# Cross-attention with a mixture-of-experts layer on one core: the value product written in head order, transfers given to other halves, four gate stores issued by ScalarE

## The reference

```python
q = (lat @ Wq) * scale                       # lat: layer norm of x, 64 queries a sequence
k, v = kv_in @ Wk, kv_in @ Wv                # kv_in: 64 context rows and the 64 rows of lat
alphas = softmax(where(mask, q @ k.T, -inf)) # per sequence and head
x = x + (alphas @ v).reshape(...) @ Wo
scores = sigmoid(norm(x) @ gate_w)           # top 2 of 8, normalised: dense
h = silu(xt @ w1) * (xt @ w3)                # per expert
x = x + shared(xt) + sum_e dense[:, e] * (h_e @ w2_e)
```

## Time and profile before

| what | before |
|---|---|
| median of three runs | 1117.17 us (1116.64 to 1120.89) |
| the profiled execution: its own time | 1118.87 us |
| its span, first to last instruction | 1117.1 us |
| PE busy | 1076.3 us (96%) |
| DVE busy | 928.3 us (83%) |
| ACT busy | 789.0 us (71%) |
| POOL busy | 617.0 us (55%) |
| mean granted TensorE clock | 0.991 |

### The profile page before, as it was taken

How to read it: one execution, slowest core, us unless ns; L and a number is a source line. 1 busy time by engine, 2 the same in 40 slices (tenths; PEclk the granted TensorE clock), 3 DMA queues, 4 the chain that set the end, 5 groups by cost and what they waited for, 6 DMA issues and landing times.

```text
span 1117.1 us, 28209 instructions
## 1 busy us (share of the span) xinstructions
PE 1076.3 (96%) x7720; PEld 939.3 (84%) x7720; DVE 928.3 (83%) x4095; ACT 789.0 (71%) x2924; POOL 617.0 (55%) x717
## 2 busy tenths in 40 slices
PE   6899999999999999999999999999999999999986
PEld 5688888888888888888888888888888888888765
DVE  3878988888988888988888888888898888888856
ACT  4777777767777776777776777777777777777631
POOL 5554655565656565655555556556565556554421
PEclk9999999999999999999999999999999999999989
DMA  5454555555565545555555655555555554555541
GB/s 153 128 175 152 171 171 166 153 155 162 168 176 171 160 146 167 171 171 165 157 155 159 172 170 169 168 156 158 165 168 171 174 153 153 163 168 160 158 121 34
DMA packets 248717, 176.81 MB, mean 158 GB/s; under 512 B 29424, under 2 KB 215408, under 8 KB 248560
## 3 DMA queue, kind: packets, MB, share of 16 engines
q1 hardware_dynamic: 247376, 173.96, 52.6%
q10 hardware_dynamic: 1184, 1.05, 0.3%
HBM read 103.35 MB, written 71.56 MB: 157 GB/s over the span
## 4 chain that ended last, share of the span: by engine, by line
PE 61%; SPq 14%; DMA 9%; DVE 8%; issue 5%; ACT 2%; POOL 0%; DVEq 0%; POOLq 0%; ACTq 0%
PE bank L861 14%; PE bank L874 12%; PE bank L816 9%; PE bank L818 9%; PE bank L817 9%; SPq L335 8%; DMA pT<-probsT_dram 8%; PE bank L822 5%; SPq L328 2%; SPq L351 2%; DVE probsT L687 2%; DVE logits L672 1%; SPq L369 1%; ACT cT_hi L528 1%; ACT probs L558 1%
## 5 line engine op out<-in xcount | busy, mean ns | idle before, releaser
L454 POOL TENSOR_TENSOR probs<-probs,rdenom 128x512 f32<-128x512 f32 x256 | 266.7, 1042 | 339.8 <-DVE rdenom L681 335.4
L558 ACT ACTIVATE probs<-logits,neg_max 128x128 f32<-128x128 f32 x1024 | 398.8, 396 | 0.9 <-DVE neg_max L672 0.9
L874 PEld LDWEIGHTS bank<-kvT,tT 128*128 128x128 f32 x2048 | 268.9, 192 | 120.5 <-issue 102.2
L861 PE MATMUL bank<-pT,kv_f 128*128 128x512 f32 x512 | 267.5, 604 | 16.5 <-DMA pT<-probsT_dram 16.0
L874 PE MATMUL bank<-kvT,tT 128*128 128x128 f32 x2048 | 270.5, 275 | 0.0
L672 DVE CUSTOM_DVE_ANT_0 logits<-bank,mask_add 128x128 f32<-128x128 f32 x1024 | 232.5, 282 | 6.1 <-PE bank L874 5.9
L717 DVE TENSOR_TENSOR cT_lo<-bank,cT_hi 128x512 fp32r<-128x512 f32 x256 | 175.1, 684 | 60.5 <-ACT cT_hi L528 60.5
L528 ACT CAST cT_hi<-bank 128x512 fp32r<-128x512 f32 x256 | 150.1, 586 | 94.7 <-PE bank L861 94.6
L558 ACT ACTIVATION_READ_ACCUMULATOR probs<-logits,neg_max 128x1 f32 x1024 | 197.7, 193 | 0.0
L513 ACT ACTIVATE h_tanh<-bank 128x256 f32<-128x256 f32 x160 | 61.6, 385 | 179.1 <-PE bank L818 176.7
L687 DVE STREAM_TRANSPOSE probsT<-probs 128x512 f32<-128x512 f32 x256 | 175.9, 687 | 0.5 <-issue 0.5
(11 more groups left out here) (102 smaller groups left out, 1986.1 us busy)
## 6 DMA issues: line engine op xcount, KB each, us to landing
probsT_dram<-probsT SPq DMA_DIRECT2D x256, 256.0 KB, 2.2
pT<-probsT_dram SPq DMA_DIRECT2D x1024, 64.0 KB, 2.2
gates<-gates_dram SPq DMA_DIRECT2D x62, 256.0 KB, 4.2
kv_raw<-in_ctx SPq DMA_DIRECT2D x32, 128.0 KB, 2.8
kv_raw<-in_x SPq DMA_DIRECT2D x32, 128.0 KB, 2.9
mask_raw<-in_mask_BxS_ik SPq DMA_DIRECT2D x32, 128.0 KB, 3.7
x_res<-in_x SPq DMA_DIRECT2D x32, 128.0 KB, 2.6
out<-out_sb SPq DMA_DIRECT2D x32, 128.0 KB, 2.1
```

Source lines behind the costliest of these rows:

```text
L454: nc.gpsimd.tensor_tensor(by_pair, by_pair, rdenom[n][:, :].unsqueeze(2).unsqueeze(3).broadcast_to([P, PAIRS, P // QUAD, QUAD]), ALU.mult) ...
L558: nc.scalar.activation(probs[c % 4][:, :, r, :], logits[c % 2][:, r, :].rearrange("p (c k) -> p c k", k=QUAD), ACT.Exp, bias=neg_max[c % 2 ...
L861: nc.tensor.matmul(C_ps[c % 2][:, :], kv_f[g % 3][:, kl % 4, :], pT[c % 3][:, :], start=True, stop=True).then_inc(C_in_psum, 1)
L874: last = nc.tensor.matmul(S_ps[c % 2][:, P * r:P * (r + 1)], tT[:, kl % 4, hd:hd + 2, :], kvT[g % 2][:, kl % 4, :], start=True, stop=True)
```

## The change

The value product is written in head order where it is copied out: the copies read the bank as before and write 32 columns at a time to their head's place, so that a head's 64 queries are one run. The transfers of SP change their halves (key and value rows 7 to 2, mask 1 to 3, x 2 to 3, output 3 to 4, the gates' loads from half 0 of the next frame to half 7), and the four gate stores, in SP's halves 5 and 6, go to ACT's queue, to the end of half 6. The gates' loads in half 7 wait for the stores of the same frame.

```diff
         def head_columns(cT, hd):
-            hh, r, odd = hd // 8, hd % 8 // 2, hd % 2
-            return cT.rearrange("p b t (o a r q) -> p b t o a r q", o=2, a=2, r=PAIRS)[:, :, hh, odd, :, r, :]
+            return cT.rearrange("p b t (h q) -> p b t h q", h=8)[:, :, hd // 8, hd % 8, :]
+
+        def by_quad(row):
+            return row.rearrange("p (r a q) -> p a r q", r=PAIRS, q=QUAD)
...
-                    if k == 0 and has(j, p, 3, NG + 1):
-                        sp.wait_ge(gates_stored, 64 * (i - 2))
-                        after(sp, h_routed_done, NT * (i - 3))
+                    if k == 2 and has(j, p, -2, NG - 4):
+                        load_kv(j, p + 3)
+                    if k == 3 and has(j, p, -1, NG - 3):
+                        load_mask(j, p + 2)
...
+                    if k == 7 and has(j, p, 2, NG):
+                        sp.wait_ge(gates_stored, 64 * (i - 1))
+                        after(sp, h_routed_done, NT * (i - 2))
                         for a in range(2):
                             sp.dma_start(gates[FH * a:FH * (a + 1), :, :],
...
-                    if k in (5, 6) and has(j, p, 2, NG):
-
-                        sp.wait_ge(gate_step, GATE_STEPS * (i - 1))
-                        after(sp, gates_loaded, 32 * (i - 2))
-                        for a in (0, 1) if k == 5 else (2, 3):
-                            sp.dma_start(gates_dram.rearrange("e (t a q) -> e t a q", t=TT, a=P // QUAD)[:, :, a, :],
-                                         g_denseT[QUAD * a:QUAD * a + E, :, :]).then_inc(gates_stored, 16)
...
-                        nc.scalar.copy(cT_hi[g % 2][:, kl % 4, kl // 4, :], C_ps[c % 2][:, :]).then_inc(cT_hi_ready, 1)
+                        nc.scalar.copy(by_quad(cT_hi[g % 2][:, kl % 4, kl // 4, :]),
+                                       C_ps[c % 2][:, :].rearrange("p (a r q) -> p a r q", r=PAIRS, q=QUAD)).then_inc(cT_hi_ready, 1)
...
+                    if k == 6 and has(j, p, 2, NG):
+                        act.wait_ge(gate_step, GATE_STEPS * (i - 1))
+                        after(act, gates_loaded, 32 * (i - 2))
+                        for a in range(P // QUAD):
+                            nc.scalar.dma_start(gates_dram.rearrange("e (t a q) -> e t a q", t=TT, a=P // QUAD)[:, :, a, :],
+                                                g_denseT[QUAD * a:QUAD * a + E, :, :]).then_inc(gates_stored, 16)
...
-                        nc.vector.tensor_tensor(cT_lo[g % 2][:, kl % 4, kl // 4, :], C_ps[c % 2][:, :],
-                                                cT_hi[g % 2][:, kl % 4, kl // 4, :].bitcast(fp32),
+                        nc.vector.tensor_tensor(by_quad(cT_lo[g % 2][:, kl % 4, kl // 4, :]),
+                                                C_ps[c % 2][:, :].rearrange("p (a r q) -> p a r q", r=PAIRS, q=QUAD),
+                                                by_quad(cT_hi[g % 2][:, kl % 4, kl // 4, :].bitcast(fp32)),
                                                 ALU.subtract).then_inc(cT_lo_ready, 1)
...
-                            last = matmul3(W_ps.rearrange("p (b a q) -> p b a q", b=GB, a=2), MV_hi[1][:, hd, :], MV_lo[1][:, hd, :],
+                            last = matmul3(W_ps.rearrange("p (b q) -> p b q", b=GB), MV_hi[1][:, hd, :], MV_lo[1][:, hd, :],
```

More of the change, by code:

```diff
@@ L346, in frame @@
                         load_probs(e - 2)
-                    if k == 0 and has(j, p, 3, NG + 1):
-                        sp.wait_ge(gates_stored, 64 * (i - 2))
-                        after(sp, h_routed_done, NT * (i - 3))
+                    if k == 2 and has(j, p, -2, NG - 4):
+                        load_kv(j, p + 3)
+                    if k == 3 and has(j, p, -1, NG - 3):
+                        load_mask(j, p + 2)
+                    if k == 3 and has(j, p, 0, NG - 1):
+                        after(sp, x1_step, 3 * (i - 2) + 1)
+                        sp.dma_start(x_res[p][:, :, :],
+                                     x.rearrange("b s d -> (b s) d")[bass.ds(GT * i, GT), :].rearrange("(t q) d -> q t d", q=P)
+                                     ).then_inc(x_res_loaded[p], 16)
+                    if k == 4 and has(j, p, 4, NG + 2):
+                        store_out(i - 1)
+                    if k == 7 and has(j, p, 2, NG):
+                        sp.wait_ge(gates_stored, 64 * (i - 1))
+                        after(sp, h_routed_done, NT * (i - 2))
                         for a in range(2):
@@ L353, in frame @@
                                          ).then_inc(gates_loaded, 16)
[L354 to L363, removed]
-                    if k in (5, 6) and has(j, p, 2, NG):
-                        sp.wait_ge(gate_step, GATE_STEPS * (i - 1))
-                        after(sp, gates_loaded, 32 * (i - 2))
-                        for a in (0, 1) if k == 5 else (2, 3):
-                            sp.dma_start(gates_dram.rearrange("e (t a q) -> e t a q", t=TT, a=P // QUAD)[:, :, a, :],
-                                         g_denseT[QUAD * a:QUAD * a + E, :, :]).then_inc(gates_stored, 16)
-                    if k == 7 and has(j, p, -2, NG - 4):
-                        load_kv(j, p + 3)
                 if i == NG + 2:
```

## The result

The change takes 1110.82 us, the median of six runs (1109.57 to 1114.02); the kernel before, on the same chip, 1119.06 (1116.64 to 1122.62). The ratio is 0.9927, 95% interval 0.9906 to 0.9947: 8.2 us less, where 11.0 were forecast (1106 us, from the 1117.17 of the first three runs of before). The profiled execution took 1111.61 us with a span of 1109.8, 7.3 less than before.

A forecast was written before the change was run, and what follows sets the result against it. PE was taken to bound the kernel, with a steady wait for pT. Terms -11.7 - 1.5 - 3 + 4.0 + 1.2 = -11.0 us, from 1117.2 to 1106 us; range 1100 to 1119.

The forecast's parts named there:

- The gates' loads (-11.7): Gate loads moved to half 7 no longer delay half 1's pT; PE's whole wait for pT goes, -11.7 us.
- ScalarE's stores (0): Four gate stores on ACT, 2.94 us, start ahead of half 6's exponentials, so half 7's copy tT stays in time: price 0.
- Rivals 1 and 2: ACT's stores wait in order behind the exponentials: 1115 us at 0.70 us an issue (0.11), or dearer, 1131 us (0.12).
- rival 1: ACT's stores wait in order behind the exponentials, at 0.70 us an issue: +9.2, 1115 us; chance 0.11.
- 0.33 us of PE a frame, 28 frames: If stores wait for the exponentials, half 7's copy tT ends late and PE loses this much: 9.2 us.
- The break-even of 1.1 us an issue: ACT's four stores cost PE nothing in half 7 up to 1.1 us an issue, if started ahead of the exponentials.
- Rival 3: The pT wait only moves to half 2, gate loads blocking half 0's loads: 1116 us; chance 0.09.
- 1.2 to 1.9 us to spare: Margin by which half 0's pT, behind the moved gate loads, comes before PE wants it in half 2.
- Rival 4: ACT's and SP's issues take turns, four stores take 4.8 us, PE loses 0.24 us a frame: 1113 us; chance 0.05.
- The head order (-1.5): The projection's 1536 matmuls read runs of 64 instead of 32 columns: 0 to 3.1 us gained, -1.5 taken.
- The end (+2.2): Last frames: -3 from gate stores off SP, +4.0 from last stores behind ACT's tanh, +1.2 from a slower clock.
- The other moves: price 0: Key and value rows, mask and x loaded in halves 2 and 3, well before they are read: no cost.

The follow-up runs named there:

- Moves alone: The changed kernel with the value product back in the old column order, only the transfers moved: 1114.41 us, 0.9949 of the kernel before.
- Experiment 3: The changed kernel with the gates' two loads put back into half 0 of the next frame, ScalarE keeping the stores: 1118.04 us, 1.0004 of before.
- experiment 4: The changed kernel with the four gate stores back on SyncE's queue in halves 5 and 6: 1110.45 us, 0.9915 of before.
- experiment 5: The changed kernel with ScalarE's stores also waiting until the exponentials of half 6 are done: 1129.69 us, 1.0081 of before.
- Experiment 7: The changed kernel with VectorE's gate step g_keep moved behind the product h in half 4: 1103.81 us, 0.9878 of before.
- experiment 8: The changed kernel with the four gate stores of frame 32 alone issued by SyncE, in halves 5 and 6: 1103.47 us, 0.9875 of before.
- experiment 9: The kernel before, unchanged, profiled once more: 1117.11 us, a single run.
- experiment 11: The changed kernel with g_keep behind h, frame 32's stores on SyncE, and frames -2 to 0 loading in the old halves: 1096.51 us, 0.9818 of before.

## Why the prediction was right, and where it was off

**The gates' loads (-11.7) and ScalarE's stores (0): right.** Moves alone take 918.46 us for frames 3 to 30 (115.81 to 1034.27), 11.9 less than before. Experiment 3 shows that without the loads' new place the gain is gone, as the prediction argued, and experiment 4 that the queue of the stores is beside the point. That the two loads alone would give all of the 11.7 is not shown: experiment 3 puts their place at 7 to 9 us, and at 4.6 in its profiled execution. The stores start ahead of the exponentials, 0.67 to 0.69 us each in frame 13 (0.70 taken).

**Rivals 1 and 2** did not come; experiment 5 makes the queue behave as they assume, and there rival 1 was priced too low, 17 us instead of 9.2: the step "0.33 us of PE a frame, 28 frames" took frame 13 for all, and frames 2 and 3 lose several times that, frame 3 with the clock at 0.95. The break-even of 1.1 us an issue stood the test: eight issues, 5.6 us, are 1.2 us over 4.4, and the frames are 1.2 us longer. **Rival 3** did not come: between frames 3 and 31 PE has no wait for `pT` left. Its "1.2 to 1.9 us to spare" hold in most frames; in 7 of the 27 from 3 to 29 less is left, 0.65 us in the worst. Its 1116 us does not follow from the terms: without the -11.7 the others add up to +0.7, about 1118. In the same way the upper end of the sum's own bounds is -11.7 + 4.0 + 3.5 = -4.2, which is 1113 and not 1112; the measured median lies under both. **Rival 4** did not come either: it has each of ScalarE's issues take 1.19 us, and they took 0.67 to 0.69.

**The head order (-1.5) came to about -2, for another reason.** That the two are near is luck. "284 ns, the query chunk's 282: between 0 and 2 ns each" failed: the matmuls gained 7 ns, beyond what the nearest row allowed. Why they are now faster than the chunk's, no run here shows. 48 matmuls, started 114 instead of 120 ns apart, are 0.3 us a frame, 8 us in 28 frames. Of it 0.05 arrived: the wait for `h` took 0.20, a bound that the prediction did not look for, since a PE that arrives later than the product shows no wait for it. Experiment 7 gave it back, and a little more.

**The end (+2.2) measured +2.5, of larger pieces; that their sum came out so near is luck.** From frame 31 to the tanh of half 6 it gained 5.3 us (1095.96 - 1042.73 against 1080.94 - 1032.97) where -3 was taken: both the wait and the slower clock of frame 32 went. From the tanh to the expert sums it lost 5.4 instead of 4.0: the stores left 4.0 us later, as said, and the two loads landed later as well. From there to the end it lost 2.3 instead of 1.2, with the clock at 0.50 for the expert sums. In experiment 8 the late stores are gone and the end takes 69.26 instead of 76.83 us, so they cost both losses.

**"The other moves: price 0" and the first frame with gates failed by 1.1 and 1.2 us.** At the start the key and value loads stand ahead of half 5's `pT`; that this costs the 1.1 us is a guess (experiment 9), which no edit shows, as experiment 11 is too small. In frame 2 there are no expert sums yet, PE is early, and the copy behind the stores is late (PE's timeline of the full change):

```profile
115.44 0.38 PE L821 MATMUL bank<-latT_hi,MV_hi 128*128 128x256 f32 x1 [1.22 <-ACT tT L517]
```

Kernels with the stores on SyncE take 31.0 to 31.2 us for frame 2, those with four on ScalarE ahead of the exponentials 32.0 to 32.7. On SyncE the time comes back in frame 3, though (34.96 in experiment 4 against 32.74), so it is no gain to move them.

So the steps that carry the forecast held. In the two profiled executions the change gave 7.3 us, 3.7 less than the 11.0 forecast, and that is the start (2.6, of which 1.5 before the first scores, with the lower clock there) and frame 2 (1.2), which the prediction priced at nothing; the other terms together came out 0.2 us better. The medians differ by 8.2, as the profiled execution of the change lies 0.8 us above its median.

## What to carry to other kernels

When a wait sits on a load, ask first which transfer was issued just ahead of it: the place of two large loads, one half earlier or later, was worth 7 to 9 us here by the medians, while the queue that issued four small stores was worth nothing that could be measured. An instruction made shorter gives only what the next wait in line lets through, so look for the engine that was just in time before, and reorder its work around the result that is now late. A place in a queue chosen for the steady state is to be checked again in the first and last passes: in a single frame, a place behind a tanh cost 6 us.

## What the runs showed of the hardware

SyncE's issues grew beside four short issues on ScalarE's queue, but not at once. In the full change two loads issued beside the first two stores took 0.42 and 0.43 us, as without them. With the stores in order, of four loads of SyncE line 339 the first began beside the second store and took 0.38 us, and the three beside the third and fourth took 0.56, 0.61 and 0.68 (ns, minimum, median, maximum of the four):

```profile
L339 SPq DMA_DIRECT2D pT<-probsT_dram x4: 378/582/677, 483.9 to 485.6; - x4
```

and ScalarE's stayed at 0.67. The Trainium skill ("Perfetto Trace Analysis", section "DMA Instruction — HWDGE") has the descriptor block locked by one sequencer at a time; of a full alternation, in which each store would also have grown, the rows show none.
